# The high part of the next batch's context: copied by ScalarE instead of GpSimd

## What is computed

```python
q = (hidden_states @ Wq + bq).reshape(b, s, NH, HD).transpose(0, 2, 1, 3)          # 16 heads of 128
k = (encoder_hidden_states @ Wk + bk).reshape(b, se, NKV, HD).transpose(0, 2, 1, 3)  # 4 key heads
v = (encoder_hidden_states @ Wv + bv).reshape(b, se, NKV, HD).transpose(0, 2, 1, 3)
k, v = jnp.repeat(k, GROUPS, axis=1), jnp.repeat(v, GROUPS, axis=1)
q, k = _rmsnorm(q, qn_w), _rmsnorm(k, kn_w)
scores = jnp.einsum('bhsd,bhed->bhse', q, k) * scale + attention_mask[:, None, :, :]
probs = jax.nn.softmax(scores, axis=-1)
out = jnp.einsum('bhse,bhed->bhsd', probs, v)
return out.transpose(0, 2, 1, 3).reshape(b, s, NH * HD) @ Wo
```

## Time and profile before

| | |
|---|---|
| median of 3 runs | 1468.15 us (1463.97 to 1470.35) |
| the profiled execution | 1479.52 us |
| its span, first to last instruction | 1477.7 us |
| TensorE busy | 1390.1 us, 94% |
| VectorE busy | 841.9 us, 57% |
| ScalarE busy | 711.3 us, 48% |
| GpSimd busy | 611.3 us, 41% |
| mean granted clock of TensorE | 0.976 |

### The profile page before, as it was taken

One profiled execution on the slowest core, in us unless ns is written; L12 is line 12 of the kernel. 1 busy time (PEld: TensorE's weight loads), 2 busy tenths in 40 slices (PEclk: granted clock), 3 DMA queues, 4 the chain that ended last, 5 costly groups with the idle time before them and its releaser, 6 DMA issues. The chain is left out here.

```text
span 1477.7 us, 24718 instructions
## 1 busy us (share of the span) xinstructions
PE 1390.1 (94%) x8497; PEld 1174.2 (79%) x8497; DVE 841.9 (57%) x3014; ACT 711.3 (48%) x1877; POOL 611.3 (41%) x940
## 2 busy tenths in 40 slices
PE   8999999999978999999999999999999997499976
PEld 7789888888857888888888888888888876377854
DVE  4553434344356667666755765576567655744357
ACT  5755555554434444444444444454445444343246
POOL 1632211121126455545544554545454535434154
PEclk9999999999988999999999999999999999699998
DMA  6212112122334221222121212211221130765362
GB/s 202 93 38 74 59 55 73 52 68 82 132 103 120 65 60 40 65 60 59 35 77 49 70 36 66 60 59 47 65 60 51 55 117 25 260 194 169 111 220 100
DMA packets 67475, 126.56 MB, mean 86 GB/s; under 512 B 11835, under 2 KB 42911, under 8 KB 66456
## 3 DMA queue, kind: packets, MB, share of 16 engines
q1 hardware_dynamic: 62776, 110.04, 24.3%
q0 software_dynamic: 4576, 14.95, 3.6%
HBM read 93.50 MB, written 31.45 MB: 85 GB/s over the span
## 5 line engine op out<-in xcount | busy, mean ns | idle before, releaser
L1113 ACT ACTIVATE b_probs<-b_probs,b_nmax 100x361 f32<-100x361 f32 x256 | 152.6, 596 | 68.7 <-DVE b_nmax L1227 67.4
L75 PE MATMUL bank<-b_kTh,b_q 128*100 128x362 f32 x512 | 172.7, 338 | 8.6 <-POOL b_q L1391 5.3
L1370 POOL TENSOR_TENSOR b_pcarry<-b_half 128x1 f32<-128x1 f32 x173 | 37.6, 217 | 343.7 <-DVE b_rinv L1233 322.0
L1227 DVE CUSTOM_DVE_ANT_0 b_probs<-bank,b_mask 100x361 f32<-100x361 f32 x256 | 135.4, 529 | 69.4 <-issue 61.4
L1108 ACT ACTIVATE b_pTh<-bank 121x400 fp32r<-121x400 f32 x192 | 95.8, 500 | 126.5 <-PE bank L946 125.6
L1402 POOL TENSOR_SCALAR b_probs<-b_probs,b_rinv 100x361 f32<-100x361 f32 x256 | 153.7, 613 | 0.0
L1220 DVE TENSOR_TENSOR b_pTl<-bank,b_pTh 121x400 fp32r<-121x400 f32 x192 | 109.7, 572 | 38.4 <-ACT b_pTh L1108 38.3
L946 PE MATMUL bank<-ident,b_probs 100*121 100x100 f32 x768 | 111.8, 268 | 7.6 <-POOL b_probs L1402 7.0
L946 PEld LDWEIGHTS bank<-ident,b_probs 100*121 100x121 f32 x768 | 106.0, 186 | 15.3 <-POOL b_probs L1402 12.5
L75 PE MATMUL bank<-b_Woh,b_oTh 128*100 128x512 f32 x256 | 110.8, 433 | 1.4 <-DVE b_oTl L1299 1.4
L440 ACT ACTIVATE a_probs<-a_probs,a_nmax 100x100 f32<-100x100 f32 x256 | 93.2, 366 | 36.7 <-DVE a_nmax L561 36.5
(11 more groups left out here) (256 smaller groups left out, 3793.9 us busy)
## 6 DMA issues: line engine op xcount, KB each, us to landing
q_d<-a_qb SPq DMA_DIRECT2D x64, 200.0 KB, 2.4
b_q_raw<-q_d SPq DMA_DIRECT2D x64, 200.0 KB, 2.5
b_q_raw<-rs_d SPq DMA_DIRECT2D x64, 200.0 KB, 3.4
b_ctxr<-in_ctxT SPq DMA_DIRECT2D x48, 242.0 KB, 4.5
y_d<-c_y SPq DMA_DIRECT2D x32, 256.0 KB
c_Eraw<-in_expert_w SPq DMA_DIRECT2D x10, 512.0 KB, 7.4
a_stage<-in_Wq SPq DMA_DIRECT2D x4, 1024.0 KB
stage<-in_Wo SPq DMA_DIRECT2D x8, 512.0 KB, 4.5
```

Of the source, the lines that this page charges most:

```text
L75: mm = eng.matmul(out, lhsT=l(c), rhs=r(c), start=first and k == 0, stop=last and k == n - 1)
L1113: act.activation(p, p, ACT.Exp, scale=-1.0, bias=nmax[:, s % 2, h:h + 1], accum_out=psums[:, s % 2, h:h + 1]).then_inc(e_rdy, 1)
L1227: dve.tensor_tensor_reduce(out=probs[:, s % 2, h, 0:SE], in0=s_bank[h % 2][0:S, 0:SE], in1=mask_s[:], scale=-1.0, scalar=BIG, op0=ALU.add, ...
L1370: pool.tensor_tensor(pcarry[:, k:k + 1], half_s[:, 0:1], half_s[:, 0:1], ALU.add)
```

## The change

ScalarE makes the high part, in a new function `context_hi`: chunk 0 after the exponential of head 0 in quarter 1, chunk 1 after that of head 1, chunk 2 after that of head 0 in quarter 2. It waits for the load and for `v_done` as GpSimd did. GpSimd's `split_ctx` becomes `context_lo`, at the same places in its queue: it waits for the high part and subtracts. Its copy, its two waits and the carry are gone. Nothing changes on TensorE, VectorE and SyncE.

```diff
+            def context_hi(jn, c):
+                act.wait_ge(ctx_in[c % 2], ctx_loads(jn, c))
+                wait(act, v_done, 3 * (jn - 1) + c + 1)
+                act.activation(ctxh[:, c], ctxr[:, c % 2], ACT.Copy).then_inc(ctx_hi, 1)
+
...
                         if now:
                             exponent(j, s, h)
+                        if s == 1 and h < 2 and not last:
+                            context_hi(j + 1, h)
+                        if s == 2 and h == 0 and not last:
+                            context_hi(j + 1, 2)
...
-            def split_ctx(jn, c):
-                pool.wait_ge(ctx_in[c % 2], ctx_loads(jn, c))
-                wait(pool, v_done, 3 * (jn - 1) + c + 1)
-                carry_wait(c)
-                pool.tensor_scalar(ctxh[:, c], ctxr[:, c % 2], 1.0, 1.0, ALU.mult, ALU.mult).then_inc(ctx_hi, 1)
+            def context_lo(jn, c):
                 pool.wait_ge(ctx_hi, 3 * jn + c + 1)
                 pool.tensor_tensor(ctxl[:, c], ctxr[:, c % 2], ctxh[:, c].bitcast(F32),
                                    ALU.subtract).then_inc(ctx_lo, 1)
...
                     normalise(j, 0)
                     if not last:
-                        split_ctx(j + 1, 0)
-                        split_ctx(j + 1, 1)
+                        context_lo(j + 1, 0)
+                        context_lo(j + 1, 1)
                     normalise(j, 1)
                     if not last:
                         key_rsqrt(j + 1, 0)
-                        split_ctx(j + 1, 2)
+                        context_lo(j + 1, 2)
                     normalise(j, 2)
```

## The result

| | before | after |
|---|---|---|
| median of the runs | 1468.76 us (1463.97 to 1474.0, 20 runs) | 1472.83 us (1468.65 to 1478.25, 20 runs) |
| ratio, 95% interval | | 1.0023 (1.0014 to 1.0033) |
| the profiled execution | 1479.52 us | 1473.11 us |
| its span | 1477.7 us | 1471.3 us |

The account below looks back on a forecast made before the run. TensorE was taken as the bound, busy 49.75 of 50 us in cross-attention. Steady batches 0 plus batch 0's 1.2 + 0.1 = 1.3 us, added to the 1468.15 us median, gave 1469.5 us; range 1464.0 to 1475.5.

Parts of the forecast that it names:

- Steady batches, 0 us: The 14 batches after batch 0: delays stay covered and never reach TensorE, 14 x 0 = 0 us.
- The covers of 0.15 and 0.10 us: Quarter 2, steady batches: margins left before TensorE loads the first transposed key (0.15) and chunk 2's keys (0.10).
- Rival (1): Quarter 2, steady batches: a cover breaks, 0.1 to 0.3 us a batch on TensorE; 1470.9 to 1473.7 us; chance 0.22.
- Rival (2): Same place in quarter 2, further: over 0.5% slower, needing 0.43 us a batch; 1475.9 us; chance 0.09.
- The copy's price: ScalarE: each of the 45 copies of 128x484 from SBUF takes 0.60 us.
- its pitch: ScalarE: 0.53 us from one context copy's start to the next start, with ends of 0.46 and 0.99.
- The port: GpSimd's subtraction holds the shared SBUF port, delaying VectorE's query product (quarter 1) and key product (quarter 2).
- Batch 0, quarter 1: ScalarE's copies between exponentials and the held query product delay the serial chain and TensorE's wait by 1.2 us.
- the sentence on the keys of chunk 0: Loads and queues: these keys need their low part at 762.39, it is there at 760.4; cost 0.
- Quarter 2, where 0.1 was predicted: Batch 0: key product already held, subtraction moves by 0.11 us, so 0.1 us more reaches TensorE's wait.
- (3): Batch 0: TensorE's wait grows from 2.46 to about 3.0 us and slows its clock, 1.6 us; 1471.1 us; chance 0.08.

Follow-up runs that it names:

- the extra copies: The changed kernel with one more ScalarE copy before chunk 2's in the 14 steady batches: 484 columns, ratio to before 1.0059, or one column, 1.0019.
- the one-column copy: The changed kernel with one more ScalarE copy, of a single column, ahead of chunk 2's in the 14 steady batches; ratio to before 1.0019.
- the copies in gaps: The changed kernel with ScalarE's copies moved to the end of quarter 0 (chunks 0 and 1) and of quarter 1 (chunk 2); ratio to before 0.9998.
- the kernel with the busy TensorE: The changed kernel with 9 and 10 unused identity transposes on TensorE ahead of its two waits in batch 0; ratio to before 0.9986.
- the weights later on before: The kernel before, with VectorE in batch 0 splitting two output weights behind the key squares instead of ahead of them; ratio to before 0.9961.
- after with the weights later: The changed kernel, with VectorE in batch 0 splitting two output weights behind the key squares instead of ahead of them; ratio to before 0.9985.

## Why the prediction was right, and where a term was too small

**Steady batches, 0 us: right.** The period is 50.162 and 50.161 us against 50.180 and 50.174. The key product ends at 771.81 in before's frame (predicted 771.85), chunk 2's load is issued at 760.43 (760.4), and its landing is as before. The covers of 0.15 and 0.10 us are 0.18 and 0.20 by the rows and 0.13 to 0.15 by the extra copies. Rival (1) would have begun to be right with 0.2 us more on ScalarE: the one-column copy, 0.22 us, cost 1.3 us in 14 batches. Rival (2)'s place is the right one, and its price was confirmed by putting it in: 0.467 us a batch for 0.62.

**The copy's price: right, its pitch a little high.** 0.593 us against 0.60, and 0.50 between starts (771.98 to 772.48) against 0.53. The budget of the Trainium skill that the prediction took, 0.70 us, is stated there for a bias that is a pointer operand. This copy has none, and the budget was not borne out; the same page's section What ACT_TABLE_LOAD costs has, for an instruction whose scale and bias are immediates, 186 ns plus 0.833 ns an element less 93 ns of overlap, 0.589 and 0.496 us here, which agrees.

**The port: right.** The query product is held in quarter 1 and the key product in quarter 2. It does not reach TensorE in steady batches; in batch 0 it is worth 0.27 us.

**Batch 0, quarter 1: 1.2 predicted, 1.00 measured.** The queue was worked out nearly right: the probability copy and with it the query product were to be 0.86 us late, and both were 0.73 to 0.74 late. The term that was mis-sized is the end of the held query product, from which the serial chain starts: 1.19 us late in the prediction, 1.00 measured (455.31, which is 5.39 us behind the mark, against 4.39 in before). It was to end 0.55 us after GpSimd's subtraction, a figure taken from the key product of 121x512; the query product of 128x400 ended 0.42 us after it. That is 0.13 of the 0.19 us; the subtraction itself ended 0.06 us earlier than predicted. A second step failed without moving this sum, the sentence on the keys of chunk 0. Their low part was compared with its due time in a steady batch, "it is there at 760.4", and not in batch 0, where chunk 0's copy starts at 451.50 only and TensorE stands still for 0.57 us. So TensorE came to its wait for the probabilities 1.0 us later too, and that wait did not grow from 2.46 to 3.0 us: it stayed at 2.46. Quarter 2, where 0.1 was predicted, added 0.02 (13.01 against 12.99, both with an early stretch).

**The clock: a rival at 0.08 that took place, by another route.** I had given (3) the condition that the wait grows. It didn't, and the second stretch came all the same, in six of six traces with copies between the exponentials of batch 0 and the old order of the weights (TensorE not kept busy); four of four without them, the copies in gaps among them, have one. Its price was put at 1.6 us and is 1.0, or 1.5 to 1.6. What I took from one trace of before as a property of a 2.46 us wait (no stretch) was the draw of one execution, and a second trace has it the other way round. Serial 1.0 and a stretch of 1.0 to 1.5 make 2.0 to 2.5 us against the 3.4 (2.1 to 4.9) of the timings. That the range held owes something to luck: it was wide enough for a stretch that the forecast itself left out.

**What stays open.** Why two stretches come with the copies and one without them. The waits are 2.46 and 2.90 us in after and 2.46 and 2.88 in the second trace of before, yet the latter ran at 1.00 behind its 2.88. The same for 1.82 and 1.83 us, with and without. Why the stretch of the last batch lies where it does. And some 2.5 us in the timing of the kernel with the busy TensorE, some 2 in that of the weights later on before, and 1.6 between before and after with the weights later.

## What to carry to other kernels

Check each cover separately in the first and the last pass of a loop: a moved step is free in the steady batches and on the path in the one that does extra work. When a producer is moved to a busier queue, list everybody who waits for it there, not only the one who waited last before. And before long waits of TensorE are priced, take a second trace: the clock behind them may differ from one execution to the next.

## What the runs showed of the hardware that I had not expected

- After waits of 2.4 to 3.5 us in batch 0 TensorE ran at 1.2 GHz for some 3 us (the windows of 2.4 to 3.0 us shown above lie inside such stretches), or it did not: behind the same 2.46 us both occur, and behind 1.8 us, too (twice with, once without). The clock fell only when TensorE was at work again, 0.2 to 1.5 us after the wait ended. The Trainium skill, TensorE: Matmul & The Clock Gate, section Part 1: The HAM clock gate (the "warmup" mystery), says that the monitor is not started with the kernel and that the cold part varies from run to run. The two traces of before agree; no run here explains why after has two stretches each time.
- A stretch cost 1.0 us where it stood ahead of a long wait for VectorE, which became 0.6 us shorter (2.90 and 2.88 against 3.46), and 1.5 to 1.6 us where the next wait stayed at its 1.20.
- A one-column copy on ScalarE costs 0.187 us, and the next start is 0.22 us later, of the 0.593 of a full copy of 484 columns.
